# ScalarE's looks at low halves, spread over the quarters by a table of its operations

## The chip, the cores and the metric
The kernel runs on one core of a Trainium2 chip. The metric is the device time of one execution in microseconds (us). Engines are named as in the profile: PE is TensorE, DVE is VectorE, ACT is ScalarE, POOL is GpSimd, SP is SyncE.

## The reference
A decoder layer with three parts, each followed by a layer norm: self-attention (16 heads of 128, weights as 4-bit codes times a scale for each 32 rows), cross-attention in which each row keeps its 54 highest of 1024 scores, and a gated feed-forward of width 2048. Two batches of 512 rows of 512 floats.

```python
def mxfp4(x, codes, scales):
    return x @ (codes * repeat(scales, 32, axis=0))
q, k, v = (mxfp4(x, w, s) + b for w, s, b in ...)   # then 16 heads
attn = softmax(q @ k.T / sqrt(128))
x = layernorm(x + mxfp4(attn @ v, wo, so) + bo)
x = layernorm(x + xattn(x, ctx, W_qkv, W_o))        # top 54 of 1024
x = layernorm(x + (silu(x @ Wg.T) * (x @ Wu.T)) @ Wd.T)
```

## The kernel before
Every operand of a matmul is kept as two halves: a high half that ACT writes by a copy to fp32r, and a low half, which is the float32 value less the high half. A product is the sum of high by high, high by low and low by high. A weight that is a code times a scale may fit the high half exactly; then its low half is all zero, and the matmuls with it are left out at run time.

**The look and the flag.** Whether they are left out is found out so. A *piece* is a 128x512 block of a weight: ("qk", j, a) for the query and key weights of a head, ("v", g, kt) for four heads' value weights, ("o", h, 0) for the output weights of a head. For each piece SP loads codes and scales, POOL multiplies them (`multiply`, L1951 and L1954), ACT writes the high half (`high`, L999) and POOL the low half (`low`, L1965; DVE for "v", L1471). Then ACT *looks* at the low half: `look` (L1037) takes absolute values and sums them into a column of `mag`. When all pieces of a key (2 for "qk" and "o", 4 for "v") are looked at, POOL reduces the column to one number, the flag (`low_total`, L1970). TensorE's program loads the flag into a register (`load_flag`, L617) just ahead of the first matmul that belongs to it and branches around the matmuls with the low half (L682, L703, L740). The four engines wait for one another by semaphores: the look for the low half and for the look before it, the total for its last look, the load for the total.

**The quarters.** Self-attention is one loop over i = 0 to 127 on every engine, written out by hand. I call step i "quarter i", or Qi: j = i // 4 is a head of one batch, qt = i % 4 a tile of 128 rows of its scores. In a quarter TensorE does, in this order: for qt < 2 the query or key projection of the next head (first matmul L678, with flag ("qk", j+1) loaded for qt = 0); for qt = 0 the product with the values of the head before (`attend`, L723); for qt >= 2 a tile of the output projection (`proj_o`, L739, flag ("o", p) at the first tile); in some quarters a tile of the value projection (`proj_v`, L700, flag ("v", g)); four transposes (L713); and the scores of Q(i+2) (L656, L658, L660). ACT does in Qi, in this order, what answers to it: `qk_high` L1011, `ot_high` L1047, `o_scale` L1058, `v_high` L1017, `pt_high` L1043, the exponential of Q(i+2) L1024, then the quarter's looks, then the quarter's `high`s, and from Q114 on pieces of the next stage (`conv_xw`, L1078). POOL does in Qi: the totals of the quarter, one addition into `acc` where ACT scaled the tile (L2068), the low halves of the pieces of Q(i-2), the multiplies of the pieces of Qi, bias additions (L1979), and from Q114 on its part of `conv_xw` (L1983).

`LOOKS` says which pieces ACT looks at in which quarter, `TOTALS` in which quarter POOL makes a flag, `LOWCOL` the column of a key. All three come from `low_plan`, which the change rewrites. The order of the two engines around them:

```python
for key in TOTALS.get(i, []):      # POOL, first in quarter i
    low_total(key)
...
exponential(i + 2)                 # ACT, quarter i
for piece in LOOKS.get(i, []):
    look(piece)
```

Of the kernel before, what the change touches and what calls it, by code (L numbers as in the profile page):

```python
# [24 lines left out]
NJ = 32  # L25
HB = [(2 * p + i, b) for p in range(6) for b in range(2) for i in range(2)]
# [109 lines left out]
def o_tile(i):  # L136

    j, qt = divmod(i, 4)
    return (j // 2 - 1, 2 * (j % 2) + qt - 2) if qt >= 2 and j >= 2 else None
# [17 lines left out]
def pieces_at(i):  # L157

    j, qt = divmod(i, 4)
    out = []  # L160
    if j % 8 in (4, 5) and qt < 2 and j < 24:
        out.append(("v", j // 8 + 1, 2 * (j % 8 - 4) + qt))
    if qt in (1, 2) and j + 3 < NJ and WJ[j + 3] == j + 3:
        out.append(("qk", j + 3, qt - 1))
    if qt >= 2 and (j % 4 == 0 and j < 28 or j == 26):
        out.append(("o", (j // 2 if j < 24 else j - 12) + qt - 2, 0))
    return out
# [5 lines left out]
def low_key(piece):  # L173

    return ("o", piece[1] // 2) if piece[0] == "o" else piece[:2]


def low_size(key):
    return 4 if key[0] == "v" else 2


def low_plan():


    queue = [(-1, ("v", 0, kt)) for kt in range(4)]
    looks, totals, col, seen, full = {}, {}, {}, {}, []
    for i in range(-1, 4 * NJ):
        if i >= 0:
            for item in list(full):
                if item[0] < i:  # L190
                    full.remove(item)
                    totals.setdefault(i, []).append(item[1])
        for _ in range(2):
            if queue and queue[0][0] < max(i, 0):
                piece = queue.pop(0)[1]
                key = low_key(piece)
                col.setdefault(key, len(col))
                looks.setdefault(i, []).append(piece)
                seen.setdefault(key, []).append(piece)
                if len(seen[key]) == low_size(key):  # L200
                    full.append((max(i, 0), key))
        if i >= 2:
            queue += [(i, piece) for piece in pieces_at(i - 2)]
    return looks, totals, col, seen


# [50 lines left out]
def row_writers(r):  # L257
# [8 lines left out]
    else:  # L266
        out += ["bo2", (14, 0), (14, 1), (15, 0), (15, 1)]
    return out + ["ln1", "cross", "ln2", "ffn", "ln3"]


def scaled_by_act(q, tt, h):

    return h == 1 and (q < 13 or q == 13 and tt < 2)


def decoder_layer(nc, xT, xn, wq, sq, wk, sk, wv, sv, wo, so, bqk, bv, bo,
# [1933 lines left out]
```

## Time and profile before

| | before |
|---|---|
| median of 3 runs | 944.97 us (943.44 to 947.11) |
| the profiled execution | 945.73 us, its span 943.9 us |
| PE busy | 912.9 us, 97% of the span |
| DVE busy | 593.0 us, 63% |
| ACT busy | 575.5 us, 61% |
| POOL busy | 491.8 us, 52% |
| granted TensorE clock, mean | 0.994 |
| self-attention's quarters | about the first 515 us of the span |

Matmuls are pipelined: the profile gives one of 512 columns 0.39 us, while the next starts 0.23 us after it. So a wait of up to 0.16 us is not seen as idle time, and the idle time named by the profile is that much shorter than the wait. I read waits of PE from starts.

### The profile page before, as it was taken

The page shows a single profiled execution, that of the slowest core. Times are in us where ns is not written, and L with a number is a line of the kernel's source. Part 1 is how long each engine was busy: PE and PEld are TensorE (multiplying, and loading weights), DVE is VectorE, ACT ScalarE, POOL GpSimd, SP SyncE. Part 2 cuts the span into 40 slices and gives each one's busy share as a digit, 9 for nine tenths or more (in the row PEclk, how much of TensorE's full clock was granted, in tenths as well). Part 3 has the DMA queues.
Part 4 walks back from the last instruction along what each step waited for, and adds up shares of the span by engine and source line. Part 5 has one row for each costly group of instructions (what it writes and reads, how often), then busy time and mean ns, then how long its engine had stood idle before and what let it go on. Part 6 is the DMA issues. An engine that isn't in the chain of part 4 may idle for free.

```text
span 943.9 us, 13220 instructions
## 1 busy us (share of the span) xinstructions
PE 912.9 (97%) x4440; PEld 750.1 (79%) x4440; DVE 593.0 (63%) x1066; ACT 575.5 (61%) x1142; POOL 491.8 (52%) x407
## 2 busy tenths in 40 slices
PE   8999999999999999999989889899999899999997
PEld 7788788887888877887868678798878788888885
DVE  5666966669666686658694899975878125411114
ACT  4667876678766787778874366533755534443333
POOL 4357752556526466477743467534764741354440
PEclk9999999999999999999999999899999999999999
DMA  7531230212302223123112303323433331343321
GB/s 202 157 104 53 86 89 1 61 58 75 100 1 54 64 74 84 46 72 86 54 43 83 90 23 101 104 76 100 124 91 99 104 112 41 112 122 94 94 83 44
DMA packets 46102, 76.97 MB, mean 82 GB/s; under 512 B 5584, under 2 KB 11216, under 8 KB 45776
## 3 DMA queue, kind: packets, MB, share of 16 engines
q1 hardware_dynamic: 45600, 75.68, 27.2%
q8 instruction: 40, 0.66, 0.3%
q10 hardware_dynamic: 432, 0.39, 0.2%
q14 instruction: 30, 0.25, 0.1%
HBM read 73.69 MB, written 2.36 MB: 81 GB/s over the span
## 4 chain that ended last, share of the span: by engine, by line
PE 40%; DVE 8%; ACT 2%; issue 2%; POOL 1%; ACTq 0%; DVEq 0%; POOLq 0%
PE p L895 6%; PE p L896 6%; PE p L899 6%; PE p L909 3%; PE p L910 3%; PE p L911 3%; DVE m L1561 1%; PE p L861 1%; PE p L862 1%; PE p L863 1%; PE p L776 1%; PE p L774 1%; PE p L773 1%; DVE acc L1522 1%; DVE st L1529 1%
## 5 line engine op out<-in xcount | busy, mean ns | idle before, releaser
L1983 POOL TENSOR_TENSOR V<-RAW,V 128x512 fp32r<-128x512 f32 x64 | 82.4, 1309 | 142.1 <-ACT V L1078 142.1
L1496 DVE TENSOR_SCALAR_CACHE_REDUCE JK<-p,ssc 128x512 bf16<-128x512 f32 x112 | 83.7, 747 | 112.9 <-PE p L660 112.9
L1024 ACT ACTIVATE PR<-p,nms,ssc 128x512 f32<-128x512 f32 x112 | 87.5, 781 | 60.0 <-DVE JK L1496 58.7
L2068 POOL TENSOR_TENSOR acc<-SX,acc 128x512 f32<-128x512 f32 x54 | 69.8, 1293 | 75.0 <-ACT SX L1058 51.8
L678 PE MATMUL p<-R 128*128 128x512 f32 x248 | 97.3, 392 | 0.8 <-DVE V L1489 0.8
L1983 POOL TENSOR_TENSOR C<-RAW,C 128x512 fp32r<-128x512 f32 x58 | 76.1, 1325 | 41.2 <-ACT C L1078 41.2
L1813 DVE TENSOR_TENSOR SX<-p,SX 128x512 f32<-128x512 f32 x32 | 22.1, 691 | 116.0 <-PE p L899 109.9
L1509 DVE TENSOR_TENSOR PT<-p,PT 128x512 fp32r<-128x512 f32 x128 | 87.4, 683 | 5.4 <-ACT PT L1043 5.2
L713 PEld LDWEIGHTS p<-ident,PR 128*128 128x128 f32 x512 | 62.4, 140 | 21.2 <-DVE PT L1509 6.6
L713 PE MATMUL p<-ident,PR 128*128 128x128 f32 x512 | 77.4, 274 | 1.0
L1043 ACT ACTIVATE PT<-p 128x512 fp32r<-128x512 f32 x128 | 75.8, 592 | 0.7 <-PE p L713 0.7
L680 PE MATMUL p<-R 128*128 128x512 f32 x192 | 75.1, 391 | 0.0
L1333 ACT ACTIVATE C<-SX 128x512 fp32r<-128x512 f32 x32 | 20.2, 632 | 76.3 <-DVE SX L1813 76.3
L656 PE MATMUL p<-QK 128*128 128x512 f32 x128 | 58.1, 454 | 0.0
L1951 POOL TENSOR_TENSOR RAW<-RAW,SCL 128x512 f32<-128x512 f32 x37 | 50.1, 1354 | 14.0 <-DMA RAW<-in_wk 7.9
L739 PE MATMUL p<-WO,OT 128*128 128x512 f32 x128 | 53.8, 420 | 2.8 <-DVE acc L1522 2.4
L678 PEld LDWEIGHTS p<-R 128*128 128x128 f32 x248 | 46.6, 188 | 11.8 <-issue 1.5
L1522 DVE SCALAR_TENSOR_TENSOR acc<-p,ri,acc 128x512 f32<-128x512 f32 x74 | 54.2, 734 | 1.5 <-PE p L742 0.9
L1970 POOL CROSS_LANE_REDUCE flag<-mag 128x1 f32<-128x2 f32 (+1 forms) x30 | 9.6, 320 | 85.7 <-ACT JA L1037 85.7
L895 PE MATMUL p<-V 128*128 128x512 f32 (+1 forms) x144 | 53.1, 376 | 0.6 <-POOL V L1983 0.6
L723 PE MATMUL p<-PT,V 128*128 128x512 f32 x128 | 50.5, 394 | 2.6 <-ACT PT L1043 2.6
L896 PE MATMUL p<-V 128*128 128x512 f32 (+1 forms) x144 | 52.6, 372 | 0.0
(243 smaller groups left out, 2735.9 us busy)
## 6 DMA issues: line engine op xcount, KB each, us to landing
RAW<-in_wg SPq DMA_DIRECT2D x32, 256.0 KB, 2.9
RAW<-in_wu SPq DMA_DIRECT2D x32, 256.0 KB, 2.7
RAW<-in_ctxn SPq DMA_DIRECT2D x32, 256.0 KB, 2.8
RAW<-in_wd SPq DMA_DIRECT2D x32, 256.0 KB, 2.8
RAW<-in_wq SPq DMA_DIRECT2D x19, 256.0 KB, 2.7
RAW<-in_wk SPq DMA_DIRECT2D x18, 256.0 KB, 2.7
RAW<-in_wv SPq DMA_DIRECT2D x16, 256.0 KB, 2.8
RAW<-in_wo SPq DMA_DIRECT2D x16, 256.0 KB, 4.7
```

Source lines behind the costliest of these rows:

```text
L678: e.matmul(ps, wh[:, kt], xh[:, kt], start=kt == 0, stop=False)
L680: e.matmul(ps, wh[:, kt], xl[:, kt], start=False, stop=False)
L713: m = e.transpose(ps[:, cols(kt)], PR[:, i % 2, cols(kt)], ident[:, :])
L895: e.matmul(ps, wl[:, cols(kt)], X3[b][:, 0, kt, c], start=kt == 0, stop=False)
L896: e.matmul(ps, wh[:, cols(kt)], X3[b][:, 0, kt, c], start=False, stop=False)
L1024: e.activation(PR[:, i % 2, :], P[i % 2][:, :], ACT.Exp, bias=nms[:, i % 4:i % 4 + 1], scale=ssc[:, 0:1] if HB[j][0] > 1 else SC, accum_ou ...
L1043: e.activation(PT[:, 0, :, cols(qt)], quad(P[2 + i % 2][:, :]), ACT.Copy).then_inc(*pt_hi.up(i))
L1496: e.tensor_scalar(JK[:, :], P[i % 2][:, :], ssc[:, 1:2] if HB[i // 4][0] > 1 else -SC, None, ALU.mult, ALU.min, accum_out=nms[:, i % 4:i % ...
L1509: e.tensor_tensor(PT[:, 1, :, cols(qt)], quad(P[2 + i % 2][:, :]), PT[:, 0, :, cols(qt)], ALU.subtract).then_inc(*pt_lo.up(i))
L1522: e.scalar_tensor_tensor(out=acc[:, r], in0=P[BANK["o", q, tt, h]][:, :], scalar=ri[:, 4 * (j % 4) + tt:4 * (j % 4) + tt + 1], in1=acc[:, ...
L1983: e.tensor_tensor(lo, RAW[:, slot[key], :], hi, ALU.subtract).then_inc(*c_lo.up(key))
L2068: e.tensor_tensor(acc[:, r], OBUF[:, (4 * q + tt) % 2], acc[:, r], ALU.add).then_inc(*rows[r].up((q, 1)))
```

## The change
The looks are no longer taken two a quarter from a queue in the order of the pieces. A table `ops` holds how many operations ACT has in each quarter. Each piece of Qi gets the quarter with the fewest operations in the window from Q(i+3) to two quarters ahead of its flag's first use (of equals the later one), and the table is counted up. The total stays in the quarter after the last look of its key. Columns are numbered anew in the order of the looks. `scaled_by_act` only moves up in the file, so that every later line number grows by 12.

```diff
+def act_ops(i):
+
+    j, qt = divmod(i, 4)
+    n = 2 + (qt < 2) + (qt == 0 and j > 0) + bool(v_tile(i)) + (len(pieces_at(i - 1)) if i else 0)
+    return n + (o_tile(i) is not None and scaled_by_act(*o_tile(i), 1))
+
+def flag_use(key):
+
+    kind, n = key
+    if kind == "qk":
+        return 4 * (n - 1)
+    return min(i for i in range(4 * NJ) if (
+        v_tile(i) and v_tile(i)[0] == n if kind == "v" else o_tile(i) and HB[2 * o_tile(i)[0]][0] == 2 * n))
...
-    queue = [(-1, ("v", 0, kt)) for kt in range(4)]
-    looks, totals, col, seen, full = {}, {}, {}, {}, []
...
-        for _ in range(2):
-            if queue and queue[0][0] < max(i, 0):
-                piece = queue.pop(0)[1]
...
-        if i >= 2:
-            queue += [(i, piece) for piece in pieces_at(i - 2)]
+    ops = [act_ops(i) for i in range(4 * NJ)]
+    for i in range(4 * NJ):
+        for piece in pieces_at(i):
+            window = range(i + 3, min(flag_use(low_key(piece)) - 2, 4 * NJ - 1) + 1)
+            at = min(window, key=lambda x: (ops[x], -x))
+            ops[at] += 1
+            looks.setdefault(at, []).append(piece)
+    for i in sorted(looks):
+        for piece in looks[i]:
...
+            if len(seen[key]) == low_size(key) and i >= 1:
+                totals.setdefault(i + 1, []).append(key)
```

TensorE's, VectorE's and SyncE's programs stay as they are. The 68 looks stay; for these flags the last look moves, or gets another place in its quarter:

| flag | its last look, before | now | first use by PE |
|---|---|---|---|
| o0 | Q6 | Q8 | Q10 |
| qk4, qk5 | Q9, Q13 | Q10, Q14 | Q12, Q16 |
| qk12, qk13 (and qk20, qk21) | Q41, Q45 (Q73, Q77) | Q42, Q46 (Q74, Q78) | Q44, Q48 (Q76, Q80) |
| qk28, qk29, qk30, qk31 | Q105, Q109, Q113, Q117 | Q106, Q110, Q114, Q118 (both looks) | Q108, Q112, Q116, Q120 |
| qk9 (and qk17) | Q29 (Q61) | Q30 (Q62) | Q32 (Q64) |
| o1 (and o3, o5) | Q22 (Q54, Q86) | Q24 (Q56, Q88) | Q26 (Q58, Q90) |
| o2 (and o4), o6, o7 | Q38 (Q70), Q102, Q110 | Q40 (Q72), Q104, Q112 | Q42 (Q74), Q106, Q114 |
| v1 (and v2, v3) | Q24 (Q56, Q88) | the same, as third look | Q26 (Q58, Q90) |

The first place, on ScalarE, is Q40 to Q42, before: L1024 is the exponential, L1037 a look, L999 a `high`, L1058 `o_scale`.

```order
L1024 ACTIVATE PR,rs<-p0,nms,ssc 128x512 [waits s_smax]
L1037 ACTIVATE JA,mag<-R1 128x512 [waits s_low_abs,s_w_lo_p]
L1011 ACTIVATE QK<-p4,bqk_t 128x512 [waits s_proj]
L1043 ACTIVATE PT<-p3 128x4x128 [waits s_ptr]
L1024 ACTIVATE PR,rs<-p1,nms,ssc 128x512 [waits s_smax]
L1037 ACTIVATE JA,mag<-R1 128x512 [waits s_low_abs,s_w_lo_p]
L1058 ACTIVATE SX0<-p6,ri 128x512 [waits s_row6,s_recip,s_oproj]
L1043 ACTIVATE PT<-p2 128x4x128 [waits s_ptr]
L1024 ACTIVATE PR,rs<-p0,nms,ssc 128x512 [waits s_smax]
L999 ACTIVATE R1<-RAW 128x512 [waits s_mul_p]
```

And now, where the look is L1049 and every other line is 12 higher:

```order
L1036 ACTIVATE PR,rs<-p0,nms,ssc 128x512 [waits s_smax]
L1049 ACTIVATE JA,mag<-WO 128x512 [waits s_low_abs,s_w_lo_p]
L1023 ACTIVATE QK<-p4,bqk_t 128x512 [waits s_proj]
L1055 ACTIVATE PT<-p3 128x4x128 [waits s_ptr]
L1036 ACTIVATE PR,rs<-p1,nms,ssc 128x512 [waits s_smax]
L1049 ACTIVATE JA,mag<-R1 128x512 [waits s_low_flag,s_low_abs,s_w_lo_p]
L1070 ACTIVATE SX0<-p6,ri 128x512 [waits s_row6,s_recip,s_oproj]
L1055 ACTIVATE PT<-p2 128x4x128 [waits s_ptr]
L1036 ACTIVATE PR,rs<-p0,nms,ssc 128x512 [waits s_smax]
L1049 ACTIVATE JA,mag<-R1 128x512 [waits s_low_abs,s_w_lo_p]
L1011 ACTIVATE R1<-RAW 128x512 [waits s_mul_p]
```

The look at the second piece of qk12 moved from ahead of Q42's `o_scale` to behind Q42's exponential; a look at an "o" piece stands in Q40 in its place.

The same stretch on GpSimd, before: L1970 is the total, L2068 the addition into `acc`, L1951 the multiply.

```order
L1965 TENSOR_TENSOR R1<-RAW,R1 128x512 [waits s_proj,s_w_hi] x2
L1951 TENSOR_TENSOR RAW<-RAW,SCL 128x512 [waits s_scl_in2,s_raw_in2]
L1970 TENSOR_REDUCE flag<-mag 1x1 [waits s_low_abs]
L2068 TENSOR_TENSOR acc<-SX0,acc 128x512 [waits s_row0,s_oscl]
L1951 TENSOR_TENSOR RAW<-RAW,SCL 128x512 [waits s_scl_in3,s_raw_in3]
L2068 TENSOR_TENSOR acc<-SX0,acc 128x512 [waits s_row1,s_oscl]
L1965 TENSOR_TENSOR R1<-RAW,R1 128x512 [waits s_proj,s_w_hi] x2
```

And now:

```order
L1977 TENSOR_TENSOR R1<-RAW,R1 128x512 [waits s_proj,s_w_hi] x2
L1982 TENSOR_REDUCE flag<-mag 1x1 [waits s_low_abs]
L1963 TENSOR_TENSOR RAW<-RAW,SCL 128x512 [waits s_scl_in2,s_raw_in2]
L2080 TENSOR_TENSOR acc<-SX0,acc 128x512 [waits s_row0,s_oscl]
L1963 TENSOR_TENSOR RAW<-RAW,SCL 128x512 [waits s_scl_in3,s_raw_in3]
L1982 TENSOR_REDUCE flag<-mag 1x1 [waits s_low_abs]
L2080 TENSOR_TENSOR acc<-SX0,acc 128x512 [waits s_row1,s_oscl]
L1977 TENSOR_TENSOR R1<-RAW,R1 128x512 [waits s_proj,s_w_hi] x2
```

The total of qk12 stood ahead of Q42's addition and multiply, and stands now behind both. (The one at the head of this piece is the total of o2.)

The second place on ScalarE is from Q23's exponential to the first operation of Q25, before:

```order
L1024 ACTIVATE PR,rs<-p1,nms,ssc 128x512 [waits s_smax]
L1037 ACTIVATE JA,mag<-WV 128x512 [waits s_low_abs,s_w_lo_d]
L999 ACTIVATE R1<-RAW 128x512 [waits s_mul_p]
L1011 ACTIVATE QK<-p6,bqk_t 128x512 [waits s_proj]
L1047 ACTIVATE OT<-p7 128x512 [waits s_av]
L1043 ACTIVATE PT<-p2 128x4x128 [waits s_ptr]
L1024 ACTIVATE PR,rs<-p0,nms,ssc 128x512 [waits s_smax]
L1037 ACTIVATE JA,mag<-WV 128x512 [waits s_low_abs,s_w_lo_d]
L1037 ACTIVATE JA,mag<-R1 128x512 [waits s_low_flag,s_low_abs,s_w_lo_p]
L1011 ACTIVATE QK<-p4,bqk_t 128x512 [waits s_proj]
```

And now:

```order
L1036 ACTIVATE PR,rs<-p1,nms,ssc 128x512 [waits s_smax]
L1049 ACTIVATE JA,mag<-WV 128x512 [waits s_low_flag,s_low_abs,s_w_lo_d]
L1049 ACTIVATE JA,mag<-WV 128x512 [waits s_low_abs,s_w_lo_d]
L1011 ACTIVATE R1<-RAW 128x512 [waits s_mul_p]
L1023 ACTIVATE QK<-p6,bqk_t 128x512 [waits s_proj]
L1059 ACTIVATE OT<-p7 128x512 [waits s_av]
L1055 ACTIVATE PT<-p2 128x4x128 [waits s_ptr]
L1036 ACTIVATE PR,rs<-p0,nms,ssc 128x512 [waits s_smax]
L1049 ACTIVATE JA,mag<-WV 128x512 [waits s_low_abs]
L1049 ACTIVATE JA,mag<-WO 128x512 [waits s_low_abs,s_w_lo_p]
L1049 ACTIVATE JA,mag<-WV 128x512 [waits s_low_abs,s_w_lo_d]
L1023 ACTIVATE QK<-p4,bqk_t 128x512 [waits s_proj]
```

Q22 (ahead of this piece) has lost its look, Q23 has two in place of one, and Q24 three in place of two: two at "v" pieces with the one at the "o" piece between them; the look at a "qk" piece has moved on to Q25. On GpSimd the totals of o1 and v1 now stand one behind the other, at the head of Q25.

## Rows read from the trace of the kernel before

**Rows 1.** Waits of PE, whole span: engine, line, releaser: us in total, times, longest.
```profile
PE p L747 <- DVE acc L1540: 4.0, 4, 1.3
PE p L723 <- ACT PT L1043: 2.6, 5, 0.6
```

**Rows 2.** Timeline at 36 us: start, us, engine, line, operation [idle before].
```profile
36.01 0.32 POOL L1970 CROSS_LANE_REDUCE flag<-mag 128x1 f32<-128x4 f32 x1 [9.85 <-ACT JA L1037]
...
36.92 0.47 PE L700 MATMUL p<-WV,R 128*128 128x512 f32 x1
```

**Rows 3.** Timeline, Q41 to the first matmul of Q44.
```profile
191.84 0.19 ACT L1037 ACTIVATION_READ_ACCUMULATOR JA<-R 128x1 f32 x1
...
192.11 0.32 POOL L1970 CROSS_LANE_REDUCE flag<-mag 128x1 f32<-128x2 f32 x1 [5.80 <-ACT JA L1037]
...
193.95 1.30 POOL L1951 TENSOR_TENSOR RAW<-RAW,SCL 128x512 f32<-128x512 f32 x1
...
193.95 0.39 PE L678 MATMUL p<-R 128*128 128x512 f32 x1
```

**Rows 4.** The flag load L617 from 192 to 194 us: ns min/median/max, first and last start.
```profile
L617 PEldq TENSOR_LOAD <-flag x1: 300/300/300, 192.6 to 192.6; - x1
```

**Rows 5.** Timeline, Q46 and the first matmul of Q48.
```profile
206.18 0.78 ACT L1024 ACTIVATE PR<-p,nms,ssc 128x512 f32<-128x512 f32 x1
...
207.01 0.39 PE L678 MATMUL p<-R 128*128 128x512 f32 x1
```

**Rows 6.** Timeline, POOL in Q10 and Q14, PE's first matmuls of Q12, Q16.
```profile
74.37 0.40 PE L678 MATMUL p<-R 128*128 128x512 f32 x1
74.53 1.30 POOL L1951 TENSOR_TENSOR RAW<-RAW,SCL 128x512 f32<-128x512 f32 x1
...
87.26 1.31 POOL L1979 TENSOR_TENSOR acc<-acc,BO 128x512 f32<-128x512 f32 x1
87.36 0.39 PE L678 MATMUL p<-R 128*128 128x512 f32 x1
```

**Rows 7.** Timeline, from Q24's product with the values to Q26.
```profile
116.93 0.50 PE L723 MATMUL p<-PT,V 128*128 128x512 f32 x1 [0.61 <-ACT PT L1043]
...
121.92 0.78 ACT L1024 ACTIVATE PR<-p,nms,ssc 128x512 f32<-128x512 f32 x1 [0.84 <-DVE JK L1496]
...
123.48 0.63 ACT L1037 ACTIVATE JA<-R 128x512 bf16<-128x512 f32 x1
...
123.91 0.39 PE L739 MATMUL p<-WO,OT 128*128 128x512 f32 x1
```

**Rows 8.** Timeline, POOL in Q106, Q114, Q118; PE's first matmuls of Q108, Q116, Q120.
```profile
431.98 0.39 PE L678 MATMUL p<-R 128*128 128x512 f32 x1
...
433.23 1.29 POOL L1954 TENSOR_TENSOR RAW<-RAW,SCL 128x512 f32<-128x512 f32 x1
...
460.18 0.39 PE L678 MATMUL p<-R 128*128 128x512 f32 x1
...
461.34 1.29 POOL L1983 TENSOR_TENSOR WV<-RAW,WV 128x512 fp32r<-128x512 f32 x1 [0.44 <-ACT WV L1078]
...
473.26 0.47 PE L678 MATMUL p<-R 128*128 128x512 f32 x1
...
475.28 1.28 POOL L1983 TENSOR_TENSOR WV<-RAW,WV 128x512 fp32r<-128x512 f32 x1 [2.33 <-ACT WV L1078]
```

**Rows 9.** Timeline, PE after its waits at 532 and 731 us.
```profile
534.02 0.50 PE L739 MATMUL p<-WO,OT 128*128 128x512 f32 x1 [1.93 <-DVE acc L1522]
...
734.13 1.26 PE L845 MATMUL p<-ident,SX 128*128 128x128 f32 x8 [2.60 <-DVE SX L1572]
```

**Rows 10.** Stretches: length, busy us (xcount) of PE, PEld, DVE, ACT, POOL, granted clock, DMA.
```profile
535.00:540.00 5.00, 4.82 (x18) 3.20 (x18) 4.09 (x9) 0.30 (x1) 1.65 (x2) 1.00 0.57 165
...
735.00:739.00 4.00, 4.00 (x13) 3.21 (x12) 0.00 (x0) 3.58 (x6) 4.00 (x5) 0.57 0.03 11
739.00:745.00 6.00, 6.00 (x28) 4.91 (x27) 1.39 (x2) 2.42 (x5) 1.61 (x2) 1.00 0.10 38
```

More of the change, by code:

```diff
@@ L179, in low_size, with scaled_by_act @@
     return 4 if key[0] == "v" else 2
-def low_plan():
-    queue = [(-1, ("v", 0, kt)) for kt in range(4)]
-    looks, totals, col, seen, full = {}, {}, {}, {}, []
[L187 to L192, printed above, removed]
-        for _ in range(2):
-            if queue and queue[0][0] < max(i, 0):
-                piece = queue.pop(0)[1]
[L196 to L201, printed above, removed]
-        if i >= 2:
-            queue += [(i, piece) for piece in pieces_at(i - 2)]
+def scaled_by_act(q, tt, h):
+    return h == 1 and (q < 13 or q == 13 and tt < 2)
+def act_ops(i):
[8 more added lines that the diff above has]
+        v_tile(i) and v_tile(i)[0] == n if kind == "v" else o_tile(i) and HB[2 * o_tile(i)[0]][0] == 2 * n))
+def low_plan():
+    looks, totals, col, seen = {-1: [("v", 0, 0), ("v", 0, 1)], 0: [("v", 0, 2), ("v", 0, 3)]}, {1: [("v", 0)]}, {}, {}
+    ops = [act_ops(i) for i in range(4 * NJ)]
[7 more added lines that the diff above has]
+        for piece in looks[i]:
+            key = low_key(piece)
+            col.setdefault(key, len(col))
+            seen.setdefault(key, []).append(piece)
+            if len(seen[key]) == low_size(key) and i >= 1:
+                totals.setdefault(i + 1, []).append(key)
     return looks, totals, col, seen
@@ L268, in row_writers @@
     return out + ["ln1", "cross", "ln2", "ffn", "ln3"]
-def scaled_by_act(q, tt, h):
-    return h == 1 and (q < 13 or q == 13 and tt < 2)
 def decoder_layer(nc, xT, xn, wq, sq, wk, sk, wv, sv, wo, so, bqk, bv, bo,
```

## The prediction

> **What bounds the kernel now.** I read the page first, for the busy shares: TensorE is at 97%, no other engine above 63%. Then the chain that ended last, which in self-attention runs over PE, and the waits by engine: ACT holds PE up seldom. Its largest share is five waits at L723, for the high half of the last transposed tile, 2.6 us in all and 0.6 the longest [rows 1]. So PE is the bound of self-attention and goes through its quarters (Q0 to Q127) almost without a gap. Whoever lightens ACT here can win about 3 us at most; whoever makes PE wait pays in full, since nothing later in the span stands idle to take it up.
>
> The wait that the change touches is not in that list, because so far it always ended in time: TensorE loads a flag before the matmuls that may be branched over. I read three views for it. First, how long the way is from the total to the matmul when nothing else delays it: at 36 us POOL starts the total at 36.01, and PE, which has run dry, starts the first matmul behind the flag at 36.92 [rows 2]. That is **0.91 us**. Second, how early a flag comes where PE doesn't wait: the total of qk12 starts at 192.11 and ends at 192.43, the load starts at 192.6 [rows 4], and the matmul behind it at 193.95 [rows 3]. Without any wait ahead of it that matmul could have started at 192.11 + 0.91 = 193.02, so there are 0.93 us to spare. Third, what the total waits for: the look's second row, 191.84 to 192.03, then 0.08 us, then the total [rows 3]. The flag thus hangs on ACT's looks with under 1 us of slack, and a quarter of the short kind (scores, a tile of the output projection, transposes) lasts about 2.1 us.
>
> **The change, step by step.** No work is added or removed: 68 looks before and after. What counts is when each flag is ready. I take the quarter of the last look from the two orders, the time of that quarter's exponential from the trace, and add: a look follows the exponential's start by 0.77, a second one in the same quarter by 1.56 (121.92 to 123.48 [rows 7]), and ends 0.73 after its own start (0.63 and a read of 0.19 that overlap by 0.09 [rows 3, 7]), the total starts 0.07 later if POOL is free, and the matmul 0.91 after that.
>
> *qk12 and qk20.* The last look moves behind Q42's exponential. But the total also moved behind Q42's addition and multiply on POOL, and that multiply runs from 193.95 to 195.25 [rows 3], which is later than the look's end (for qk13, below, where ACT alone sets it, the loss is smaller by 0.55). Matmul at 195.25 + 0.91 = 196.16 in place of 193.95: 2.2 us lost. The place repeats with the same distances for qk20: 2 x 2.2 = 4.4. (The flags o2 and o4, first used two quarters earlier, come late by about 0.5 as well, but that is inside these 2.2, since the multiply doesn't move with it.)
>
> *qk4, qk5.* The same at 74: multiply 74.53 to 75.83, matmul at 76.74 in place of 74.37: 2.4. At 87 it is the bias addition, to 88.57; 89.48 in place of 87.36: 2.1 [rows 6].
>
> *qk13 and qk21.* No multiply in Q46, so ACT sets it: 206.18 + 0.77 + 0.73 + 0.07 + 0.91 = 208.66 against 207.01 [rows 5]: 1.65, twice, 3.3.
>
> *qk9, qk17.* Here the quarter between has a value tile, 8 matmuls of 0.23 us more, which covers 1.8. Nothing.
>
> *o1, o3, o5 with v1, v2, v3.* First a gain: Q22's look is gone, 0.61 us of ACT, and PE's matmul at 116.93 comes 0.6 us earlier [rows 7]; everything behind it too. ACT's exponential in Q24 starts at 121.31, the look at the "o" piece is the second, so it ends at 121.31 + 1.56 + 0.73 = 123.60; total at 123.67, first matmul of Q26 at 124.58. Before: 123.91 [rows 7]. Net 0.67 lost, gain counted; three such places, 2.0. The value flag comes 0.8 later and is needed 0.9 later: hidden.
>
> *qk28 (and o6).* POOL has two multiplies in Q106, the second from 433.23 to 434.52; matmul at 435.43 in place of 431.98 [rows 8]: 3.45, and the doubled look in Q104 pushes what precedes by about 0.3: 3.75.
>
> *qk29.* As qk12, 2.2, less the wait of about 0.65 at L723 [rows 1] that PE now spends at the flag: 1.5.
>
> *qk30.* Between Q114's looks and Q115's total POOL now has its share of the next stage's weights, L1983, which waits for ACT's L1078; ACT has a look more ahead of that. 461.34 + 1.29 + 0.61 + 0.91 = 464.15 against 460.18 [rows 8]: 4.0.
>
> *qk31.* Both looks are in Q118 now, in front of ACT's L1078 (0.79 + 0.62). L1983 ended at 476.56, now 477.97; matmul at 478.88 against 473.26 [rows 8]: 5.6. That covers waits that came later, 0.6 at L723 and about 1.0 of the 1.3 at L747 (the layer norm's rows, whose chain starts before) [rows 1]: 4.0.
>
> **Sum:** 4.4 + 2.4 + 2.1 + 3.3 + 2.0 + 3.75 + 1.5 + 4.0 + 4.0 = 27.4 us.
>
> **The clock.** Behind the wait of 1.93 us that ended at 534.02 the granted clock stayed at 1.00, the level of 2.4 GHz; behind the wait of 2.60 us that ended at 734.13 comes a stretch with a granted clock of 0.57, which is the lower level, 1.2 GHz, for most of it [rows 9, 10]: 13 matmuls in 4 us, where the next 6 us have 28 [rows 10]. At the later rate 4 us hold 18.7, so the stretch lost 5.7 x 0.21 = 1.2 us. The two longest new waits (4.0 and 5.6 at qk30 and qk31) exceed 2.60. I take 1.2 to 1.8 for each, 3 us together. The Trainium skill (TensorE: Matmul & The Clock Gate, "HAM oscillation — how this bites in real kernels") says that a matmul stream that is broken by long waits resumes at half clock every time; the waits of this trace agree for 2.60 and not for 1.93. [...]
>
> 945.73 (the profiled execution) + 27.4 + 3 = 976.1. That execution lies 0.8 over the median of the runs shown, so against the median: 975.
>
> **The bounds of the unknown.** The 0.91 is from one place. It can't be less than the total's 0.32 and the load's 0.30 [rows 2, 4]; with 0.72, the 13 places give 2.5 us less. If POOL's work could be done earlier than I think, the look alone sets the flag, and 0.55 less is lost at four places and 1 to 1.5 at four more: 7 us less. Without any drop of the clock, 3 less. Lower end 963. On the other side the clock: six more places at 1.2 to 2.4 each, 7 to 14 more.
>
> **The rivals.**
> 1. *The table levels ACT and the flags are in time.* Then the looks taken out of Q20, Q22 and so on give the gain of [rows 1]: 0.6 at each of three or four places, at most 2.6 us, 942 to 943. For it: TensorE's program is dispatched far ahead, and loads stand early in it. Against it: the load at 192.6 starts 0.17 after its total's end, so it does wait for it [rows 3, 4]. It decides if the way from look to matmul were under 0.8 us instead of 1.7. 5%.
> 2. *The same waits, and the clock falls at the shorter ones as well:* 975 + 7 to 14 = 982 to 989. For it: 2.2 to 2.5 lies between 1.93 and 2.60 [rows 9]. 20%.
> 3. *Half the price:* the flags are late, but the engines, which all catch up while PE stands, give it back afterwards (DVE's and ACT's later waits end sooner), and the load is short: 955 to 963. Against it: PE has next to no later waits in self-attention that could be given back [rows 1]. 13%.
> 4. *Only the crowded quarters matter,* and the flags' lateness is mostly hidden: within 0.5% of before or a little above, 945 to 955. 7%.
> The forecast itself, 963 to 982: 55%.
>
> **Numbers.** 975; the range 960 to 989 leaves out rivals 1 and 4 and part of 3. No change that this kernel's measurement can tell is one within 0.5%. Slower by over 0.5%: 55 + 20 + 13 and half of rival 4, 91%. Same: 6%, mostly rival 1 and the rest of 4. Faster by over 0.5%: rival 1 would need more than it can give, 3%.
>
> **What would show it.** PE's rows: a gap ahead of the first L690 (L678 before) of Q12, Q16, Q44, Q48, Q76, Q80, Q108, Q112, Q116, Q120, of 2.4, 2.1, 2.2, 1.65, 2.2, 1.65, 2.5 to 3.5, 2.2, 3.5 to 4, 5.6 us; and ahead of Q26's first tile, 1.2 us. Each flag load within 0.2 us after its total's end. In Q43 the total starts right behind the multiply. The waits at L723 in Q24, Q56 and Q88 nearly gone. The second slice of the page's clock line stays whole, and the nineteenth to twenty-first drops. I am wrong if PE starts those matmuls before the total has ended, or if the gaps are there and the span isn't longer.

## The result, and the profile after

The changed kernel takes 980.7 us (median of 4 executions, 979.6 to 984.4) where the kernel before, run beside it, takes 945.5 (4 executions). The ratio is 1.037, with a 95% interval of 1.034 to 1.040: slower, as forecast, and 5.7 us more than the 975 of the prediction, inside its range. The profiled execution of the changed kernel took 979.59 us and its span is 977.8, 33.9 longer than before.

The head of the page after: busy time, and the clock row (40 slices of 24.4 us).

```profile
PE 920.7 (94%) x4440; PEld 752.3 (77%) x4440; DVE 597.4 (61%) x1066; ACT 578.3 (59%) x1142; POOL 491.4 (50%) x407
PEclk9999999999999999999989999989999999999999
```

PE is busy for 920.7 us where it was 912.9, and its idle time in the span grows from 31.0 to 57.1 us: 26 of the 34 us are waiting. The other 8 are matmuls that the profile shows longer, most of them at half clock behind the waits (below). The lines of self-attention are 12 higher than before: L690 is the old L678, L751 the old L739, L672 the old L660. PE's waits, longest sums first, which answer to [rows 1]:

```profile
PE p L690 <- POOL flag L1982: 22.5, 10, 5.4
...
PE p L751 <- POOL flag L1982: 4.2, 4, 1.1
PE p L672 <- DVE QK L1494: 3.2, 5, 0.7
```

The first two rows are new and make 26.7 us: ten waits ahead of projections and four ahead of the output projection, all for a flag. The third grew from 0.8 us; that one I hadn't foreseen. The waits at L723 (now L735) are gone, as predicted. The fourteen flag waits are each 0.16 us longer than the profile names them. Three more, ahead of the first output tile of Q42, Q74 and Q114 (flags o2, o4 and o7), are of 0.4 to 0.46 us; the profile puts what it sees of them, 0.8 us in three, down to "issue".

The place of [rows 3] after the change, Q42 to the first matmul of Q44 (timeline: start, us, engine, line, operation, idle time before):

```profile
200.58 1.28 POOL L1963 TENSOR_TENSOR RAW<-RAW,SCL 128x512 f32<-128x512 f32 x1
...
201.11 0.19 ACT L1049 ACTIVATION_READ_ACCUMULATOR JA<-R 128x1 f32 x1
...
201.80 0.32 POOL L1982 CROSS_LANE_REDUCE flag<-mag 128x1 f32<-128x2 f32 x1
...
202.63 0.47 PE L690 MATMUL p<-R 128*128 128x512 f32 x1 [1.58 <-POOL flag L1982]
```

The flag load of this place is the answer to [rows 4]:

```profile
L629 PEldq TENSOR_LOAD <-flag x1: 298/298/298, 202.2 to 202.2; - x1
```

Read it backwards. PE starts at 202.63 and the total started at 201.80, so the way is 0.83 (0.91 in the prediction). The look is read out at 201.30 (201.11 + 0.19), and the total could start then. It starts 0.50 later, as POOL's multiply of Q42 comes to its end (200.58 + 1.28; the rows overlap by 0.06): POOL is busy with its own work and the total stands behind it.

Q12 and Q16 answer to [rows 6]. The first matmul of Q12 starts at 77.20 for 74.37 before:

```profile
75.17 1.27 POOL L1963 TENSOR_TENSOR RAW<-RAW,SCL 128x512 f32<-128x512 f32 x1
...
76.40 0.30 POOL L1982 CROSS_LANE_REDUCE flag<-mag 128x1 f32<-128x2 f32 x1
...
77.20 0.47 PE L690 MATMUL p<-R 128*128 128x512 f32 x1 [2.02 <-POOL flag L1982]
...
92.25 0.47 PE L690 MATMUL p<-R 128*128 128x512 f32 x1 [1.79 <-POOL flag L1982]
```

Two of the three places of [rows 8], the flags of qk30 and qk31, with POOL's share of the next weights ahead of the total:

```profile
488.27 1.26 POOL L1995 TENSOR_TENSOR WV<-RAW,WV 128x512 fp32r<-128x512 f32 x1 [1.21 <-ACT WV L1090]
489.50 0.32 POOL L1982 CROSS_LANE_REDUCE flag<-mag 128x1 f32<-128x2 f32 x1
490.33 0.47 PE L690 MATMUL p<-R 128*128 128x512 f32 x1 [3.14 <-POOL flag L1982]
...
506.97 1.27 POOL L1995 TENSOR_TENSOR WV<-RAW,WV 128x512 fp32r<-128x512 f32 x1 [7.19 <-ACT WV L1090]
508.19 0.32 POOL L1982 CROSS_LANE_REDUCE flag<-mag 128x1 f32<-128x2 f32 x1
509.03 0.77 PE L690 MATMUL p<-R 128*128 128x512 f32 x1 [5.38 <-POOL flag L1982]
```

In both the total starts when POOL's L1995 ends, as the prediction had it, and each L1995 waits for a copy of ACT.

And Q24 to Q26, the answer to [rows 7]:

```profile
129.22 0.18 ACT L1049 ACTIVATION_READ_ACCUMULATOR JA<-WO 128x1 f32 x1
...
129.48 0.32 POOL L1982 CROSS_LANE_REDUCE flag<-mag 128x1 f32<-128x2 f32 x1 [2.53 <-ACT JA L1049]
...
130.31 0.47 PE L751 MATMUL p<-WO,OT 128*128 128x512 f32 x1 [1.05 <-POOL flag L1982]
```

Here POOL is idle, and the look alone sets the flag.

**The account of the 34 us.** I laid the two traces side by side and took, for the first matmul behind each flag, its start after less its start before, and how much that difference grows from one quarter to the next. For Q12, for example, it grows by 2.19 at that matmul. At the places the prediction named, in its order:

| place | predicted, us | grew by, us |
|---|---|---|
| Q44, Q76 (qk12, qk20) | 2.2 each | 2.15, 2.17 |
| Q12, Q16 | 2.4, 2.1 | 2.19, 1.94 |
| Q48, Q80 | 1.65 each | 1.65, 1.67 |
| Q22 to Q26 and its two repeats | 0.67 each | 1.7 each |
| Q108 | 3.75 | 3.55 |
| Q112, less the wait at L723 | 1.5 | 1.66 |
| Q116 | 4.0 | 4.07 |
| Q120, less the waits at L723 and L747 | 4.0 | 3.9 |
| half clock in self-attention | 3 | 4.9 |

Some rows hold two steps. The row for Q44 and Q76 contains the 0.41 and 0.46 that the difference grows by two quarters earlier (flags o2 and o4), that for Q108 the 1.23 at Q106 (o6), and that for Q116 the 0.65 at Q114 (o7); the steps at their own first matmuls are 1.75, 1.72, 2.44 and 3.30.

The half clock's 4.9 are some 1.7, 1.6 and 1.6 behind the waits of Q108, Q112 and Q120. The column sums to 35.0; 0.4 came before Q10 (0.2 of it ahead of the first quarter), and behind self-attention the kernel is 1.7 shorter, which leaves the 33.9 within 0.2.

### The profile page after: what moved, and what is told of

Its sections match the earlier page's. It is cut to its first block, busy times and chain, and to the rows that moved or that the text cites. A ratio compares the mean times of both kernels' runs of the same rounds, so it can differ in the third digit from the quotient of the medians.

```text
span 977.8 us, 13213 instructions
## 1 busy us (share of the span) xinstructions
PE 920.7 (94%) x4440; PEld 752.3 (77%) x4440; DVE 597.4 (61%) x1066; ACT 578.3 (59%) x1142; POOL 491.4 (50%) x407
## 4 chain that ended last, share of the span: by engine, by line
PE 77%; DVE 11%; issue 5%; ACT 4%; POOL 2%; DMA 1%; SPq 0%; ACTq 0%; POOLq 0%; DVEq 0%
PE p L907 6%; PE p L908 6%; PE p L911 6%; PE p L690 5%; PE p L725 4%; PE p L692 4%; PE p L735 3%; PE p L736 3%; PE p L739 3%; PE p L712 3%; PE p L921 2%; PE p L923 2%; PE p L922 2%; PE p L672 2%; PE p L670 2%
## 5 line engine op out<-in xcount | busy, mean ns | idle before, releaser
L1995 POOL TENSOR_TENSOR V<-RAW,V 128x512 fp32r<-128x512 f32 x64 | 82.4, 1310 | 141.1 <-ACT V L1090 141.1
L690 PE MATMUL p<-R 128*128 128x512 f32 x248 | 99.9, 403 | 23.3 <-POOL flag L1982 22.5
L1995 POOL TENSOR_TENSOR C<-RAW,C 128x512 fp32r<-128x512 f32 x58 | 76.1, 1326 | 40.4 <-ACT C L1090 40.4
L690 PEld LDWEIGHTS p<-R 128*128 128x128 f32 x248 | 47.4, 191 | 37.9 <-issue 27.7
L692 PE MATMUL p<-R 128*128 128x512 f32 x192 | 76.4, 398 | 0.0
L751 PE MATMUL p<-WO,OT 128*128 128x512 f32 x128 | 54.7, 427 | 7.6 <-POOL flag L1982 4.2
L668 PE MATMUL p<-QK 128*128 128x512 f32 x128 | 58.2, 454 | 0.0
L672 PE MATMUL p<-QK 128*128 128x512 f32 x128 | 51.2, 400 | 3.2 <-DVE QK L1494 3.2
L1023 ACT ACTIVATE QK<-p,bqk_t 128x512 fp32r<-128x512 f32 x64 | 43.6, 681 | 17.7 <-PE p L697 12.8
L907 PE MATMUL p<-V 128*128 128x512 f32 (+1 forms) x144 | 52.1, 369 | 0.7 <-POOL V L1995 0.7
L754 PE MATMUL p<-WO,OT 128*128 128x512 f32 x128 | 51.8, 405 | 0.0
```

The source lines that it names most:

```text
L672: e.matmul(ps, QK[:, s, 0, 0, c], QK[:, s, 1, 1], start=False, stop=True).then_inc(*score.up(i))
L690: e.matmul(ps, wh[:, kt], xh[:, kt], start=kt == 0, stop=False)
L692: e.matmul(ps, wh[:, kt], xl[:, kt], start=False, stop=False)
L907: e.matmul(ps, wl[:, cols(kt)], X3[b][:, 0, kt, c], start=kt == 0, stop=False)
L1995: e.tensor_tensor(lo, RAW[:, slot[key], :], hi, ALU.subtract).then_inc(*c_lo.up(key))
```

## The experiments

**Does the whole loss run over the flags?** Two runs (e1 and e2) take the flags out of TensorE's program, in either order of looks: no load, no wait, no branch, and the products with the low halves that hang on a flag are left out for good. ACT and POOL do all their work as before.

```diff
             def load_flag(reg, key):
-                w.wait_ge(*low_flag.at(key))
-                c = LOWCOL[key]
-                e.load(regs[reg], flag[0:1, c:c + 1].bitcast(I32))
+                pass
...
-                    with e.If_ne(regs["qk"], 0):
-                        for kt in range(4):
-                            e.matmul(ps, wl[:, kt], xh[:, kt], start=False, stop=False)
```

(and the same for "v" and "o".)

> The kernel before without the flag loads and the branches on TensorE; the products with the low halves of the flagged weights are left out for good (all of them are skipped at run time before, too). Looks, totals and their order stay as before. Theory A (flags are in time before the change, and cost TensorE nothing): 941 to 946 us. Theory B (the loads and branches themselves hold TensorE up): under 938.

Measured: 946.4 us, ratio to before 0.9998 (0.998 to 1.001). The flags cost the kernel before nothing.

> The changed kernel with the same parts left out: no flag loads, no branches, no products with the flagged low halves; looks and totals in the changed order. Theory A (the loss is TensorE waiting for late flags): within 4 us of the run without flags of the kernel before, so 941 to 949, what is left being the look's effect on other engines (the 0.85 us that VectorE loses in Q22, Q54 and Q86, less the 0.6 won at the product with the values). Rival C (crowded quarters of ScalarE, or the order of ScalarE and GpSimd as such): it stays near 970 to 980, since ScalarE and GpSimd do the same work in the same order.

Measured: 948.8 us, ratio 1.0038 (1.0017 to 1.0059). All but 3 us of the 35 is gone: the flags carry the loss. PE's waits say where the rest lies:

```profile
PE p L670 <- DVE QK L1484: 3.4, 5, 0.9
...
PE p L727 <- ACT PT L1045: 2.0, 2, 1.8
```

The five waits for DVE's QK, of which the kernel before has two (0.8 us), stay when no flag is waited for, so they are a second, separate effect. Laid beside the trace without flags of the kernel before, each of Q22, Q54 and Q86 loses 0.83 to 0.85 and wins 0.60 to 0.62 two quarters later, 0.7 for the three. There is a third effect, which the waits for the flags cover in the changed kernel, and it does run through ACT. In Q120 PE waits for the high half of the transposed tile, which stands behind both looks of Q118 (the second of them is the first row):

```profile
476.68 0.63 ACT L1039 ACTIVATE JA<-R 128x512 bf16<-128x512 f32 x1
...
477.83 0.57 ACT L1045 ACTIVATE PT<-p 128x512 fp32r<-128x512 f32 x1
...
478.45 0.50 PE L727 MATMUL p<-PT,V 128*128 128x512 f32 x1 [1.82 <-ACT PT L1045]
```

The difference grows by 1.38 there, and 0.57 comes back at Q121: 0.8. By the end of self-attention the two traces without flags differ by 2.2; the rest of it lies in smaller steps.

**One quarter more for each flag** (e3). The table is kept, but the window in which it may put a look ends one quarter earlier.

```diff
-            window = range(i + 3, min(flag_use(low_key(piece)) - 2, 4 * NJ - 1) + 1)
+            window = range(i + 3, max(i + 3, flag_use(low_key(piece)) - 3) + 1)
```

> The changed kernel with the window of each look ended three quarters ahead of the flag's first use in place of two (two for the last value pieces, which have no other place). The table and the count of operations stay; ScalarE's quarters are crowded by up to three looks as after the change. Theory A: the waits at the query and key projection are gone, and the time is that of before within 4 us, 942 to 949. Rival C (crowding): 955 or more, since the looks of a key now stand in one short quarter.

Measured: 949.1 us, ratio 1.0029 (1.0015 to 1.0042). No wait at L690 for a flag is left, and again some waits for QK are:

```profile
PE p L672 <- DVE QK L1494: 2.5, 4, 0.7
```

So the levelling of ACT by a table isn't what costs. The last quarter that it was allowed is.

**POOL's part of it** (e4). The changed kernel with the total of a "qk" flag in the quarter of its last look, ahead of POOL's multiply, and not first in the next quarter. `LATE(key)` is true for every other flag.

```diff
-                totals.setdefault(i + 1, []).append(key)
+                totals.setdefault(i + (0 if key[0] == "qk" and key[1] > 3 else 1), []).append(key)
...
+                for key in TOTALS.get(i, []):
+                    if not LATE(key):
+                        low_total(key)
                 for piece in pieces_at(i):
                     multiply(piece)
```

> The changed kernel with GpSimd's totals of the query and key flags in the quarter of their last look, ahead of that quarter's multiply (and ahead of conv_xw), in place of the head of the next quarter. Theory A with GpSimd's share as I worked it out: the wait at Q44 and Q76 falls from 2.2 to 1.65, at Q108 from 2.5 to 1.4, at Q116 from 3.3 to about 0.7, at Q120 from 5.5 to about 3.7: 7 us less before the clock, 968 to 974. Rival D (the look alone sets the flag, GpSimd's place is of no matter): 979 to 982.

Measured: 976.2 us, ratio 1.0315 (1.0289 to 1.0342), span 971.2, 6.6 less than the changed kernel's. The waits:

```profile
PE p L695 <- POOL flag L1987: 14.2, 9, 3.6
PE p L677 <- DVE QK L1499: 4.6, 6, 1.7
```

The flag waits at this line fall from 22.5 to 14.2 and two thirds of them stay. The larger part of the lateness is thus ACT's look itself, the smaller what POOL has ahead of the total. Place by place (steps at the first matmul alone): the step ahead of Q44 is 1.32 in place of 1.75, ahead of Q12 1.72 in place of 2.19, ahead of Q120 3.74 in place of 5.50, and ahead of Q116 it nearly goes, 0.49 in place of 3.30. It is not a clean removal. The steps at the flags are 7.9 us smaller in all, and the half clock behind Q108 and Q112, 3.2 us, is missing in this profile; against them the wait for QK grew by 1.4, and new steps of 1.2 and 2.9 stand at Q102 and Q110. So the 6.6 are a balance. The trace shows what stands ahead of the two new steps:

```profile
420.61 5.63 DVE L1704 SCALAR_TENSOR_TENSOR CB<-RAW,mv,CB 128x512 f32<-128x512 f32 x1
...
454.02 6.77 DVE L1704 SCALAR_TENSOR_TENSOR CB<-RAW,mv,CB 128x512 f32<-128x512 f32 x1 [1.18 <-POOL RAW L1971]
```

These are one operation each, DVE's `value_bias`, of which the shortest takes 0.74. The two took 0.96 and 1.85 in the changed kernel. Here POOL runs five operations back to back until 425.69 in the one place and five until 460.23 in the other, and each time DVE's ends 0.55 behind the last of them. It is the collision of the paragraph on QK below, at a higher price. Why DVE doesn't get in between two of POOL's operations here, as it does in the changed kernel, no run shows.

**One kind of look at a time.** The next two kernels (e5 and e6) mix the two orders: one kind of key stands where the table puts it, the other as before.

```diff
+    for plan, moved in ((old, False), (new, True)):
+        for i in sorted(plan):
+            for piece in plan[i]:
+                if i > 0 and MOVED(low_key(piece)) == moved:
+                    looks.setdefault(i, []).append(piece)
...
+def MOVED(key):
+    return key[0] == "qk"      # e5; in e6: key[0] != "qk"
```

> Only the looks of the q and k weights stand where the table puts them; those of the v and o weights stand where the kernel before has them. Theory A (the flag waits of the qk pieces and the clock make nearly all of the loss, the places add up): PE waits for the flag ahead of Q12, Q16, Q44, Q48, Q76, Q80, Q108, Q112, Q116 and Q120, about 22 us on L690's counterpart, no wait ahead of Q26's first tile, span 970 to 974 (before's plus 27 to 30). Rival (the v and o looks, which crowd Q23 to Q25, make ACT late for everything behind): span under 965.

Measured: 978.6 us (976.1 to 981.1), ratio 1.033 (1.031 to 1.036). The profiled execution has ten flag waits:

```profile
PE p L739 <- POOL flag L2031: 25.3, 10, 5.4
```

The rival is out: without one v or o look moved, the loss is nearly whole. The span, 979.3, missed 970 to 974. It was 2.4 us late by Q4 already, and PE ran at half clock behind five waits (ahead of Q16, Q108, Q112, Q116 and Q120), where the first profile of the changed kernel has three. The mix also crowds ACT in Q109 and Q110, where an "o" look of the old order now stands ahead of a look at qk29: the step at Q112 is 2.95 where the changed kernel has 2.06.

> Only the looks of the v and o weights moved; those of q and k stand as before. Theory A (each of the three places Q22 to Q26 costs the flag's 1.2 and, ahead of Q22's scores, 0.85 for DVE's value_bias that collides with POOL's low half, less 0.6 won at the high half): plus 1.5 to 1.7 at each, 5 us, and up to 2 in the last quarters; span 949 to 951. The prediction's own term (flag alone, 0.67 each): 946 to 947.5 and no gap ahead of Q22's scores. If the crowd at Q24 costs ACT more: above 953.

Measured: 959.6 us, ratio 1.013 (1.011 to 1.015). This misses the first two expectations and lies above the 953 of the third, a crowd at Q24; but the crowd is one that I built. The place Q22 grew by 0.83, as expected, but Q26 by 1.91 in place of 1.2, and the steps ahead of Q42, Q74, Q106 and Q114 are 1.2, 1.2, 1.9 and 1.15, where the changed kernel has 0.4, 0.5, 1.2 and 0.4; it was also 1.9 late by Q4, and lost 1.5 to the clock behind Q58. In the mix, qk8's look from the old order stays in Q24 with the three of the new one, and goes first: the o and v looks each come one look later. A look costs about 0.8 behind another (0.79 in the prediction's account), and 1.91 less 1.20 is 0.7. The same happens at qk12 in Q40, and at its repeats in Q72, Q104 and Q112. So e5 and e6 are not two halves that add up (32 + 13 is more than 35), and e6 shows only the sensitivity: one more look ahead of a flag that has no slack is paid by PE nearly in full (0.7 of 0.8).

**The wait for QK that nobody ordered.** In Q22 after the change (timeline):

```profile
114.15 1.31 POOL L1977 TENSOR_TENSOR WO<-RAW,WO 128x512 fp32r<-128x512 f32 x1 [0.45 <-ACT WO L1011]
...
114.42 1.58 DVE L1699 SCALAR_TENSOR_TENSOR CB<-RAW,mv,CB 128x512 f32<-128x512 f32 x1
...
116.44 1.27 POOL L1966 TENSOR_TENSOR RAW<-RAW,SCL 128x512 f32<-128x512 f32 x1 [0.99 <-DMA SCL<-in_sv]
...
116.59 0.74 DVE L1494 SCALAR_TENSOR_TENSOR QK<-p,bqk_t,QK 128x512 fp32r<-128x512 f32 x1
...
117.39 0.49 PE L672 MATMUL p<-QK 128*128 128x512 f32 x1 [0.74 <-DVE QK L1494]
```

and in the kernel before:

```profile
109.48 0.74 DVE L1687 SCALAR_TENSOR_TENSOR CB<-RAW,mv,CB 128x512 f32<-128x512 f32 x1
...
109.81 1.55 POOL L1965 TENSOR_TENSOR WO<-RAW,WO 128x512 fp32r<-128x512 f32 x1 [1.09 <-ACT WO L999]
```

It is the same pair of instructions. Before, DVE is first by 0.33 and takes 0.74. After, the look of Q20 is gone, ACT's high half is done sooner, POOL starts first, and DVE's operation takes 1.58; the maximum and the low half of Q behind it are late and PE waits. The freed look that matters for this is that of Q20, ahead of the high half in Q21, and not that of Q22, whose 0.6 us is the gain at Q24. Over all 15 instances the median of this line goes from 748 ns to 1568:

```profile
L1687 DVE SCALAR_TENSOR_TENSOR CB<-RAW,mv,CB x15: 740/748/1768, 53.9 to 440.4; 128x512 f32<-128x512 f32 x15
```

```profile
L1699 DVE SCALAR_TENSOR_TENSOR CB<-RAW,mv,CB x15: 741/1568/1849, 54.1 to 463.3; 128x512 f32<-128x512 f32 x15
```

The test cuts that operation to 8 of its 512 columns, in the changed kernel (e7) and, as a control, in the kernel before (e8). Both leave out most of the value bias.

```diff
-    e.scalar_tensor_tensor(out=CB[:, :], in0=raw, scalar=bv_f[:, h:h + 1], in1=CB[:, :],
+    e.scalar_tensor_tensor(out=CB[:, 0:8], in0=raw[:, 0:8], scalar=bv_f[:, h:h + 1], in1=CB[:, 0:8],
```

> The changed kernel with DVE's value_bias done on 8 of its 512 columns (most of the value bias is left out). Theory A (DVE's op over SBUF and POOL's op over SBUF slow each other, and that makes Q22, Q54 and Q86 late): the gap of 0.85 ahead of the scores of Q22, Q54 and Q86 goes, POOL's op beside it takes 1.3 in place of 1.75; 2.5 to 4 us less than the changed kernel, 976.5 to 978.5. Rival (QK is late there because ACT's high half is): the gap stays, 980 to 981.

Measured: 983.3 us (978.1 to 987.4), ratio 1.039 (1.034 to 1.043). That misses the 976.5 to 978.5 of the theory, but the interval also covers the changed kernel's 1.037, so the time doesn't decide. By the rows the theory stands in the main: the difference at Q22, Q54 and Q86 grows by 0.31 to 0.33, where it grew by 0.85. The profiled execution is not shorter for it because it ran at half clock behind five flag waits (ahead of Q12, Q16, Q112, Q116 and Q120), some 1.6 us each, where the first profile of the changed kernel has three (below). One row shows the mechanism more plainly than I had hoped:

```profile
117.66 1.29 POOL L1977 TENSOR_TENSOR WO<-RAW,WO 128x512 fp32r<-128x512 f32 x1 [0.83 <-ACT WO L1011]
...
117.93 1.04 DVE L1699 SCALAR_TENSOR_TENSOR CB<-RAW,mv,CB 128x8 f32<-128x8 f32 x1
```

Eight columns take 1.04 us; the shortest instance of this form takes 0.217. It ends at 118.97 and POOL's operation at 118.95. DVE doesn't share with POOL, it stands until POOL is through; the same is so at the two repeats. That is also why a remainder of 0.3 stays (1.04 less the 0.74 of before): a short operation waits as long for POOL as a long one.

> The kernel before with the same cut in value_bias: the control of the run above. Theory A: PE is not held up by DVE there, so within 0.5 us of before, 944.5 to 946. If DVE's time in these quarters costs something before too: 941 to 944.

Measured: 945.2 us, ratio 0.9985 (0.9974 to 0.9997). The time is in the range of theory A, but 1.1 under the kernel before beside it (946.4), more than the 0.5 that it allowed. The traces agree with the ratio: the difference shrinks by 0.15 behind each of Q22, Q54, Q86 and Q110 and by 0.7 within Q110, where PE's wait for QK goes: PE's waits at L660 for DVE's QK are 0.8 us in two in the kernel before and 0.3 in one in the control. So the operation is nearly, and not wholly, hidden in the kernel before: it costs some 1.2 us there, most of it in Q110. Of the 0.5 that the cut gives back at Q22 in the changed kernel, 0.15 is had in the kernel before as well.

**A version that keeps what paid** (e9). Of the whole change one thing gained: ACT without a look in Q22, Q54 and Q86. This kernel is the one before, with only that, and the same for Q110.

```diff
+                late = piece[0] == "o" and piece[1] in (3, 7, 11, 15)
-                looks.setdefault(i, []).append(piece)
+                looks.setdefault(i + late, []).append(piece)
...
-                    full.append((max(i, 0), key))
+                    full.append((max(i, 0) + late, key))
```

> The order of before, with one edit: the look at the second 'o' piece of o1, o3, o5 and o7 comes one quarter later (Q23, Q55, Q87, Q111 in place of Q22, Q54, Q86, Q110), and its total too. Theory A (the one part of the change that paid was ACT free of a look in Q22, Q54 and Q86; the flags o1, o3 and o5 have a quarter to spare, and the looks of Q20 stay, so POOL's low half doesn't start ahead of value_bias): the waits at L723's counterpart go from 2.6 to under 0.8, no flag wait, span 1.5 to 2.3 less: 943.5 to 944.5 where before is 946. Rival (the gain is given back at the next flag or at DVE): 945.5 to 946.5.

Measured: 943.6 us (12 executions) against 946.4 (17), ratio 0.9972 (0.9961 to 0.9982): 2.8 us less than the kernel before, a small gain but clear of the spread. Its span is 942.1. The difference of the traces shrinks by 0.60, 0.56, 0.57 and 0.59 at Q24, Q56, Q88 and Q112 and nowhere else grows. What is left of the waits for the transposed tile's high half, 2.6 us in five before:

```profile
PE p L724 <- ACT PT L1044: 0.4, 1, 0.4
```

The margin that it uses is visible too: PE's first tile of Q26 starts at 123.84 without a wait, 0.07 earlier than in [rows 7], though this execution was 0.55 late by Q4.

**The last two flags by themselves** (e10). MOVED(key) is now `key in (("qk", 30), ("qk", 31))`.

> Only the looks of qk30 and qk31 stand where the table puts them. Theory A: flag waits of 3.3 to 4.0 ahead of Q116 and 5.5 ahead of Q120, 1.0 given back at Q121, so 8.5 to 9 us, and 0 to 3.5 for the clock: 954 to 958. Rival (the late flags here are the work of the earlier delays, which shift PE against the weights' arrival): under 950.

Measured: 956.5 us, ratio 1.0105 (1.0084 to 1.0126), span 955.2. The rival is out. The wait ahead of Q120 is 5.39 us by the profile, and that ahead of Q116:

```profile
465.04 0.47 PE L739 MATMUL p<-R 128*128 128x512 f32 x1 [3.64 <-POOL flag L2031]
```

The growth is 3.81 at Q116 and 5.53 at Q120, each followed by 1.6 to 1.7 at half clock, and 1.03 comes back at Q121. Two late flags cost 10 us.

**The clock, in a second profile of the same kernel** (e11). Nothing is edited.

> The changed kernel unchanged, a second profiled execution. If the clock's fall hangs on the wait alone, the same quarters show half speed as in the first profile (behind the waits ahead of Q108, Q112 and Q120, not behind those ahead of Q12, Q44 and Q116) and the gaps behind them agree within 0.2 us. If it also hangs on where the wait falls, waits of the same length are followed by half speed at other places, and the span differs by some 1.5 us for each.

Measured: 980.75 us (one execution), span 979.0. Stretches of 3 us behind six of the flag waits, those ahead of Q12, Q16, Q108, Q112, Q116 and Q120 (columns: length, PE busy, matmuls, granted clock, DMA). First profile:

```profile
77.00:80.00 3.00, 2.80 (x12) 1.00 0.00 0
92.00:95.00 3.00, 2.75 (x12) 1.00 0.00 0
...
454.70:457.70 3.00, 3.00 (x9) 0.50 0.21 44
472.00:475.00 3.00, 3.00 (x9) 0.50 0.04 8
490.30:493.30 3.00, 2.97 (x13) 1.00 0.00 1
509.00:512.00 3.00, 2.97 (x7) 0.50 0.30 89
```

Second profile, the same places, moved to where they now lie:

```profile
77.00:80.00 3.00, 3.00 (x8) 0.50 0.00 0
94.00:97.00 3.00, 3.00 (x9) 0.51 0.00 0
...
457.00:460.00 3.00, 3.00 (x10) 0.61 0.08 20
473.00:476.00 3.00, 2.19 (x10) 1.00 0.01 3
...
491.50:494.50 3.00, 3.00 (x13) 1.00 0.02 3
...
510.00:513.00 3.00, 2.82 (x7) 0.50 0.33 87
```

And the matmul behind the wait ahead of Q16 in the second profile, to be read beside the one at 92.25 above:

```profile
93.47 0.47 PE L690 MATMUL p<-R 128*128 128x512 f32 x1 [1.79 <-POOL flag L1982]
```

The wait is 1.79 us in both. In one execution the granted clock stays at 1.00, the level of 2.4 GHz, in the other it falls to 0.51, that of 1.2 GHz, and PE loses 1.63 us more there. At Q112 it is the other way round, and the second profile is 1.62 us ahead. The wait makes the fall possible; which of the shorter waits is hit changes from one execution to the next. The longest is hit each time: the wait of 5.4 us ahead of Q120 is followed by half clock in both profiles and in the three other traces that have it (e5, e10 and e7). The wait ahead of Q116, 3.14 or 3.15 us, is not followed by it in these two and is in e7's. The Trainium skill (TensorE: Matmul & The Clock Gate, "What's actually happening") states that what watches TensorE's activity runs freely and doesn't start anew with a kernel, so that the point of a change varies between runs. That the place differs between executions agrees with it; that this is the reason no run here shows.

## Why the prediction was right, and where its sizes were off

The forecast was a slower kernel, by flags that come late on the way over ACT's looks and POOL's total. That is what the traces show, at the places that it named, and the time lies 5.7 us above its 975.

**The way from look to matmul** was right, and it is the core of the forecast. 0.91 was measured at 0.80 to 0.84 (76.40 to 77.20, 201.80 to 202.63, 489.50 to 490.33, 508.19 to 509.03). [Rows 2] had a total over four columns and a PE that had run dry for long; the total over four columns takes the same 0.32, and what makes the 0.08 no run shows. Ten "qk" places at about 0.08 less are 0.8 us, which covers what the "qk" terms came out under the forecast: 24.95 against 25.45 in the table.

**What POOL has ahead of the total** was right in kind at the eight places where it was counted, as the table shows. e4, which moves the total ahead of it, gave 0.4 to 0.5 back at the places of 2.2 where the bound said 0.55, and more at the crowded ones, 7.9 us in all against the bound's 7. That its span is 6.6 less is a balance of this with other things.

**Rival 1, flags in time,** is refuted by the fourteen flag waits, and e2 shows what it would have looked like: 949, not 942. Even without a flag the table doesn't win: the collision takes more than the gain at Q24 and its repeats, and both looks of qk31 in one quarter hold up ACT's high half for Q120.

**Rivals 3 and 4, lateness that is given back or hidden,** fall with the table: in self-attention no more came back than was named, 1.03 at Q121 and the waits at L723.

**The step that was mis-sized is that of o1, o3, o5 with v1, v2, v3:** "Net 0.67 lost, gain counted; three such places, 2.0". Its parts were right (the flag's 1.20 to 1.23 against 1.28, the gain 0.57 to 0.61 against 0.6), but the term had no line for DVE, and each place lost a further 0.85 ahead of Q22's scores and some 0.25 behind Q26. The places cost 5.1. The 0.25 are the first matmuls behind the wait, which start 0.31 apart in place of 0.23. I had followed the 0.6 us of Q22's look to PE, and not those of Q20's look, which is gone too: they let POOL start earlier and thereby ahead of DVE. The row that should have made me look is that of DVE's L1687: its 15 instances span 740 to 1768 ns with a median of 748, so in a few quarters something already doubled it. The Trainium skill (SBUF — State Buffer, "Who interferes with whom") says that a DVE instruction with two inputs in SBUF contends with a GpSimd instruction that reads SBUF, that the ports they share are an exclusive lock, and that the order of issue decides who blocks. The rows agree: 0.74 when DVE is first and POOL then takes 1.55 in place of 1.3; 1.58, or 1.04 for eight columns, when POOL is.

**The clock** was 4.9 for 3, with the likeliest case too low and rival 2 too high. The mechanism that I chose, a length of wait between 1.93 and 2.60 from which it falls, is wrong. e11 and the first profile show a wait of 1.79 with and without it, e10 one of 3.64 with it, the changed kernel one of 3.14 without; only the wait of 5.4 had it in every trace. The price of a single fall, 1.2 to 1.8 by the estimate from [rows 10], was right: 1.6 to 1.7. Three falls in self-attention are what the first profile had, two of them at other places than I named; the second had four. That 4.9 is no further from 3 is in part luck: e7's trace had five falls. The sign that I gave for it was wrong too. The waits ahead of Q12 and Q16 lie in the fourth slice of the page's clock line, not the second, and of the nineteenth to twenty-first only the last drops in tenths (0.86, with 0.93 in the two ahead of it).

**The sum.** For the profiled execution the prediction had 976.1, and it took 979.6. The terms fell short by 3.1 at Q22 to Q26 and by 1.9 for the clock and were 0.5 too high for "qk", 4.5 in all; with the 0.4 ahead of Q10 and the 1.7 that came back behind self-attention that leaves 3.2 of the 3.5. The median lies a further 1.1 above that execution, where the prediction had gone 0.8 down to the median of before.

## What to carry to other kernels

A table that levels an engine's load must be given due times that end at the consumer's start less the whole way there, here look 0.73, total behind whatever POOL is doing, and 0.83 to the matmul; a window that is one quarter too long cost 35 us, and one that ends a quarter earlier cost 3. When work is taken off an engine, follow the freed time to every engine that it releases: the order in which two engines reach a shared resource can turn over. And when a change makes many short waits on TensorE, judge it by the differences of its traces quarter by quarter, since the clock alone moves the total by 1.6 us a time and not at the same places twice.

## What the runs showed of the hardware that I had not expected

- An operation of DVE with both inputs in SBUF, started 0.27 us behind one of POOL that reads SBUF, ended 0.54 after POOL's and took 1.58 us for 0.74; cut to 8 of 512 columns it still took 1.04 for 0.22 and ended with POOL's.
- It can wait for a whole series: beside operations of POOL back to back the same operation of DVE took 5.63 and 6.77 us in e4, and ended 0.55 behind the last.
- An operation of DVE with one of its two inputs in PSUM wasn't held up: L1494 started at 116.59, 0.15 behind POOL's L1966, and took its usual 0.74.
- The same wait of 1.79 us ahead of Q16 was followed by a granted clock of 1.00 in one execution and of 0.51 in the next, 1.63 us apart; the wait of over 3 us ahead of Q116 was followed by 1.00 in both profiles, and by 0.73 in e7's; the wait of 5.4 us by 0.50 in all five traces that have it.
